# Six rows of 128 softmax denominators in place of three rows of 256, and one load that spreads their inverses

## The reference

```python
s = einsum('bhqd,bhkd->bhqk', q, k) / sqrt(48)          # masked where the branch has a mask
out_br = einsum('bhqk,bhkd->bhqd', softmax(s, -1), v_br)  # for each of three branches
out = sum(gate[br] * out_br)
```

## Time and profile before

| what | value |
|---|---|
| median of 3 runs | 984.56 us (983.65 to 985.37) |
| span of the profiled execution | 980.1 us |
| what lies around the span (median of the runs less span) | 4.5 us |
| TensorE matmul busy | 875.3 us, 89% of the span, 9216 instructions |
| VectorE busy | 595.7 us, 61% |
| ScalarE busy | 457.1 us, 47% |
| GpSimd busy | 204.5 us, 21% |

### The profile page before, as it was taken

One profiled execution on the slowest core, in us unless ns is written; L12 is line 12 of the kernel. 1 busy time (PEld: TensorE's weight loads), 2 busy tenths in 40 slices (PEclk: granted clock), 3 DMA queues, 4 the chain that ended last, 5 costly groups with the idle time before them and its releaser, 6 DMA issues.

```text
span 980.1 us, 22296 instructions
## 1 busy us (share of the span) xinstructions
PE 875.3 (89%) x9216; PEld 588.9 (60%) x9216; DVE 595.7 (61%) x1666; ACT 457.1 (47%) x764; POOL 204.5 (21%) x274
## 2 busy tenths in 40 slices
PE   9888798999999999999999999999988879978876
PEld 8675475566666665666566566656555555644553
DVE  5545534673688468845884588558844764653456
ACT  1003326453555355525543655356435645524754
POOL 1002100120225012401341124112411231131122
PEclk9999689999999999999999999999979999998988
DMA  7100000000000000000000001000100100030000
GB/s 198 25 7 1 1 6 23 23 23 28 23 23 23 28 23 23 23 28 23 23 23 28 7 23 39 23 1 23 39 11 26 36 23 23 23 81 23 2 1 22
DMA packets 25572, 25.84 MB, mean 26 GB/s; under 512 B 14688, under 2 KB 20576, under 8 KB 25344
## 3 DMA queue, kind: packets, MB, share of 16 engines
q1 hardware_dynamic: 25472, 24.42, 8.7%
HBM read 19.69 MB, written 4.72 MB: 25 GB/s over the span
## 4 chain that ended last, share of the span: by engine, by line
PE 58%; DVE 17%; ACT 11%; issue 6%; DMA 5%; POOL 2%; SPq 1%; POOLq 0%; DVEq 0%; ACTq 0%
PE ring L934 7%; PE pv L955 5%; PE side_a L633 5%; PE ring L889 5%; PE pv L973 4%; ACT pr L1190 4%; DVE rden L1676 3%; DMA scale<-branch_scale 3%; PE heads L879 2%; PE side_a L642 2%; PE heads L914 2%; PE ring L929 2%; DMA branch_scale<-rden 2%; PE heads L861 2%; PE ring L897 2%
## 5 line engine op out<-in xcount | busy, mean ns | idle before, releaser
L1190 ACT ACTIVATE pr<-ring 128x1024 f32<-128x1024 f32 (+1 forms) x128 | 120.9, 944 | 108.3 <-PE ring L938 61.0
L934 PE MATMUL ring<-kq 64*128 64x256 f32 (+2 forms) x1280 | 136.5, 341 | 0.7 <-ACT kq L1242 0.5
L934 PEld LDWEIGHTS ring<-kq 64*128 64x128 f32 x1280 | 96.3, 191 | 42.6 <-issue 30.8
L1234 ACT ACTIVATE kq<-ring 128x896 f32<-128x896 f32 x64 | 58.8, 919 | 85.3 <-PE ring L889 85.3
L1686 DVE SCALAR_TENSOR_TENSOR ob<-pv,all_gates,scale 128x256 f32<-128x256 f32 x96 | 46.3, 482 | 85.3 <-PE pv L973 38.4
L1661 DVE TENSOR_REDUCE toks<-heads 128x2 f32<-128x512 f32 x64 | 44.3, 692 | 84.8 <-PE heads L919 83.4
L573 POOL TENSOR_TENSOR toks<-ta,tb 128x128 f32<-128x128 f32 (+1 forms) x96 | 39.7, 434 | 180.4 <-DVE tb L1652 180.4
L1242 ACT ACTIVATE kq<-ring 128x256 f32<-128x256 f32 x64 | 24.6, 384 | 107.5 <-PE ring L897 107.0
L1676 DVE RECIPROCAL rden<-pv 128x256 f32<-128x256 f32 x32 | 56.2, 1756 | 25.5 <-PE pv L955 25.0
L536 POOL TENSOR_TENSOR oT<-ob 128x256 f32<-128x256 f32 x32 | 23.3, 727 | 226.3 <-DVE ob L1686 226.3
L889 PE MATMUL ring<-early,toks 128*128 128x128 f32 x448 | 63.5, 284 | 7.5 <-ACT pr L1190 7.4
(11 more groups left out here) (377 smaller groups left out, 1704.4 us busy)
## 6 DMA issues: line engine op xcount, KB each, us to landing
scale<-branch_scale SPq DMA_DIRECT2D x128, 96.0 KB, 2.3
branch_scale<-rden SPq DMA_DIRECT2D x32, 128.0 KB, 1.7
late<-in_late SPq DMA_DIRECT2D x1, 2158.5 KB, 8.4
xin<-in_x SPq DMA_DIRECT2D x16, 64.0 KB, 2.2
pr<-in_prep SPq DMA_DIRECT2D x1, 602.0 KB, 3.8
y<-ob SPq DMA_DIRECT2D x8, 64.0 KB, 1.9
kq<-in_masks SPq DMA_DIRECT2D x1, 480.0 KB, 8.5
toks<-in_final SPq DMA_DIRECT2D x1, 434.0 KB, 4.4
```

Source lines behind the costliest of these rows:

```text
L934: m = pe.matmul(ring[:, j, at:at + nq], kq[rows, k, key0:key0 + P], kq[rows, k, Q + q_:Q + q_ + nq], start=r % 2 == 0, stop=at > P)
L1190: act.activation(out, in_, ACT.Exp, scale=SCALE).then_inc(S("exp_done"), 1)
L1234: act.activation(kq[:, k, :], flat[:, 0:WIDE], ACT.Copy).then_inc(S("turned"), 1)
```

## The change

- `onesk` gets a column set for each branch and each half of the queries: the sum of branch `br` and half `x` goes to row `2*br + x`. The denominators of a group then stand in six rows of 128 columns, in columns 256 to 383 of the bank. Pieces of 256 columns are split in two, so a group has eight pieces (32 matmuls) in place of six (24); the number of columns streamed stays at 928 for each head.
- The reciprocal runs over 128x128 in place of 128x256, and the store writes 64 KB in place of 128 KB.
- One load in place of four: its source has four blocks (heads), each repeated 32 times, of 768 values that lie together; its target is all 128 partitions of `scale`, 384 KB as before.
- The set-up of `onesk` writes twice as many columns and three more single columns.

```diff
-        onesk = sb("onesk", [P, BR, 32])
+        onesk = sb("onesk", [P, BR, 2, 32])
...
-        rden = sb("rden", [P, T])
+        rden = sb("rden", [P, P])
...
-        scale_out = nc.dram_tensor("branch_scale", (P, T), F32, kind="Internal").ap()
+        scale_out = nc.dram_tensor("branch_scale", (P, P), F32, kind="Internal").ap()
...
-                    for j in range(4):
-                        sp.dma_start(scale[32 * j:32 * j + 32, :, :], scale_out[32 * j:32 * j + BR, :].unsqueeze(0)
-                                     .broadcast_to((32, BR, T))).then_inc(S("scale_loaded"), 16)
+                    sp.dma_start(scale[:, :, :].rearrange("p b t -> p (b t)"),
+                                 scale_out.rearrange("(j r) t -> j (r t)", j=4)[:, 0:BR * T].unsqueeze(1)
+                                 .broadcast_to((4, 32, BR * T))).then_inc(S("scale_loaded"), 16)
...
-                pieces = [(0, 0, T, 0, 0), (0, P, T, 1, 0), (1, 0, T, 0, T),
-                          (2, P, T, 1, P), (2, P, BAND, 1, 3 * P), (2, 0, P, 1, 2 * P)]
-                for i, (br, q_, end, part, a) in enumerate(pieces):
+                pieces = [(0, 0, P, 0, 0), (0, 1, P, 0, P), (0, 1, P, 1, 0), (1, 0, P, 0, T), (1, 1, P, 0, T + P),
+                          (2, 1, P, 1, P), (2, 1, WINDOW, 1, 3 * P), (2, 0, P, 1, 2 * P)]
+                for i, (br, x, n, part, a) in enumerate(pieces):
                     for j in range(4):
-                        m = pe.matmul(PV[32 * j:32 * j + 32, T + q_:T + end], onesk[:, br, :],
-                                      prob(g, j, part, a, end - q_), start=(i == 0), stop=(i == 5))
+                        m = pe.matmul(PV[32 * j:32 * j + 32, T:T + n], onesk[:, br, x, :],
+                                      prob(g, j, part, a, n), start=(i == 0), stop=(i == 7))
...
-            link(V.memset(onesk[:, :, :], 0.0))
-            V.memset(onesk[:, 0, BR:32], 1.0)
+            link(V.memset(onesk[:, :, :, :], 0.0))
+            V.memset(onesk[:, 0, 0, 2 * BR:32], 1.0)
             for br in range(BR):
-                V.memset(onesk[:, br, br:br + 1], 1.0)
+                for x in range(2):
+                    V.memset(onesk[:, br, x, 2 * br + x:2 * br + x + 1], 1.0)
...
-                V.reciprocal(rden[:, :], PV[:, T:2 * T]).then_inc(S("inverted"), 1)
+                V.reciprocal(rden[:, :], PV[:, T:T + P]).then_inc(S("inverted"), 1)
...
-                    dve.wait_ge(S("scale_loaded"), of * 256 + 64 * g + 64)
+                    dve.wait_ge(S("scale_loaded"), of * 64 + 16 * g + 16)
```

## The result

The changed kernel takes 1042.0 us (median of four runs, 1028.2 to 1047.5) against 985.0 for the kernel before; two of the four, the profiled one among them, are over 1.5% above the fastest and count as slow, and the fast runs alone give a ratio of 1.047 with a 95% interval of 1.036 to 1.057 (the two medians give 1.058). The prediction was 982.3 with a range of 966.5 to 997, so the change loses some 46 us by that ratio, 57 by the medians, where a small gain was forecast. When the changed kernel was timed again, six runs gave 1038.4 us, 52 above the kernel before of that job.

The account below looks back on a forecast made before the run. The prediction took TensorE's instruction list, with idle pieces between, as the bound. L633's -4.0, smaller changes at other waits, +1.5 for new late loads and +0.3 of TensorE work gave -2.3: span 977.8, time 982.3 us, range 966.5 to 997.

Parts of the forecast that it names:

- The mechanism chosen for the load: Merged load of the inverses: four outermost blocks go to four engines, waits mostly covered; 982.3 us, chance 0.57.
- rival B: Merged load spreads over sixteen engines and takes 2.6 us, path 5.2; 968.3 us, chance 0.26.
- store path: Store of the inverted sums, halved to 64 KB: between 0 and 0.16 us saved, 0.15 taken.
- L955 bound by columns: Denominator matmuls: same 928 columns, so eight more matmuls add 0 to 0.10 us per group, 0.01 taken.
- L633: TensorE's wait for the convolution's inputs behind the reciprocal: five pieces, 0.80 us off each, -4.0 us.
- the load at 5.3 us: Merged load on four engines: 3.9 us to move at 25.3 GB/s each plus 1.4 fixed; path 7.87 us.
- rival C: Merged load slow at 16.2 GB/s per engine, 7.5 us, path 10.1, holding the first branch; 996 to 998 us, chance 0.17.
- B's term: Load on sixteen engines: 0.97 us to move the bytes, 2.4 to 2.8 in all, 2.6 used.
- TensorE feels 31% of it: Of VectorE's 46.4 us waiting at the first branch in 21 groups, TensorE feels 14.2 us, 31%.
- 15 waits: VectorE's first-branch waits behind in-time loads; rival C adds 3.0 us to each, and 1.65 to six late ones.
- L790 evened out near 1: TensorE's six wait pieces at L790, 0 to 2.1 us before, become near 1 us each; together 0 change.
- The turning point: Path from reciprocal to first branch 0.6 us longer on the mean, load 5.5 to 5.6 us, cancels L633's 4.0 gain.

Follow-up runs that it names:

- the repeated execution: Another profiled execution of the changed kernel without edits, from the job that timed it again: span 1035.1 us; six runs there gave 1038.4 us.
- the kernel with the second store: Kernel before plus a second 128 KB store of the inverted sums to scratch and a wait for it ahead of the real store: 1056.6 us, ratio 1.068.

## Why the prediction was wrong

**Right.** The mechanism chosen for the load: four outermost blocks, four engines, against sixteen (rival B). The rule of the Trainium skill cited in the prediction ("DMA: Bandwidth & Descriptors", section "Why a DMA increments its semaphore by 16 and not by 1") agrees with the traces for four, two and sixteen blocks: 4, 2 and 16 small packets a load, and 3.8, 2.0 and 11.5 data packets under way at once on the mean. Reciprocal 0.96 as predicted, store path 0.18 shorter (0.15), L955 bound by columns (1.80), L633 by exactly the 4.0 us.

**Step 1 that failed: the load at 5.3 us.** It took 6.8. The fixed part is 1.35 + 0.7 = 2.0 and not 1.4, since that was taken from a store and from loads of a quarter of the size; the transfer runs at 20.6 GB/s per engine and not at the 25.3 of the earlier trace rows, which came from the start of the kernel. The middle of the two rates that the prediction had (25.3 and 16.2) would have been nearer. Path 9.3 in place of 7.87, nearer to the 10.1 of rival C. B's term failed in both parts too: sixteen engines land in 3.8, not 2.6, with the same fixed 2.0 and 1.8 to move the bytes in place of 0.97.

**Step 2 that failed, and the larger one: "TensorE feels 31% of it".** With the right path of 9.3 the working of rival C gives +2.2 us in 15 waits and +0.9 in six, 38 us on VectorE, 31% of that, less the gain at L633: some 993 us. Measured are 1042. The share of 14.2 in 46.4 was an average over waits that had mostly been covered; it said what the last us had cost, not what the next one would. Beyond that cover most of each further us passes on: VectorE's wait rose by 63 us and TensorE's waits on the path by 40 (23.3 to 63.1), nearly two thirds, even after the 4.0 gained at L633. Six groups whose first branch had not waited before do so now (27 in place of 21). Part of the rise falls on lines to which the sum gave nothing (L875: 11.5) or next to nothing (L597, L973). "L790 evened out near 1" was wrong with them: 2.2 to 4.4 in seven pieces.

**Step 3 was absent: the granted clock.** No term of the sum had it, though the trace before showed it. In the earlier trace rows L790's wait of 1.28 us is followed by a stretch at half clock. The window behind it in the kernel before, and one at full clock after that:

```profile
512.40:515.70 3.30, 3.30 (x20) 2.16 (x21) 2.52 (x12) 1.33 (x2) 0.80 (x2) 0.50 0.00 0
516.00:519.00 3.00, 3.00 (x33) 1.93 (x32) 1.60 (x6) 1.74 (x4) 0.00 (x0) 1.00 0.00 0
```

In the changed kernel the stretches at half clock make 156 us where they made 77 (146 in the repeated execution), and each of L790's seven waits (2.2 to 4.4 us) is followed by one of 3.4 to 13.7 us. The busy rows price it at 33 us of the 66 between the two profiled executions, 27 of 55 with the repeated one.

**The turning point** (a mean path 0.6 us longer than now) rested on the 31% and so lay too far out: at +0.5 the kernel before already loses 17 us. Rival C had the sign and the place right; its loss of 11 to 13 us was about a quarter of the measured one.

## What to carry to other kernels

Measured paths and times: with three rows 7.2 us, 985; 7.7, 1003; 9.1, 1057; 10.3, 1097; with six rows 6.5, 959 to 961; 6.6, 962; 9.0 to 9.3, 1038 to 1042; 13.4, 1193. On this kernel a path that an in-order engine waits on in nearly every group cost about its full length for each us added (0.9 to 1.1 us over 32 groups), not the share that had been felt so far; and where the bound engine is TensorE, the price of a new wait includes what the clock rows show behind waits of that length. When loads are merged, give the merged one as many outermost blocks as the old ones kept engines busy: here four blocks against sixteen is 77 us (1038.4 and 961.4 in one job).

## What the runs showed of the hardware

- A DRAM-to-SBUF load of 384 KB with four outermost blocks moved at 82 GB/s (393,216 bytes in 4.78 us), with sixteen blocks at some 216 (1.82 us from first to last packet). Two loads of two blocks each, issued one behind the other, used the same two engines: 393,216 bytes in 8.8 us, two packets at once.
- The first data packet of the single 384 KB load comes 1.3 us after the issue, with four or sixteen blocks; that of the first 96 KB load 0.94.
- The page gives no landing time for the loads on four or two engines; there the wait that ends at the branch shows it (issue to branch 6.8 us on four engines, 10.8 on two).
- A wait of TensorE of 2.2 us was followed by up to 13.7 us at half clock, and eight matmuls of waste ahead of each such wait saved 11 us of the kernel's time, some 20 in the kernel with the second store.
